# A fused gated block on one core: the feed-forward stage's operations in another order, the clip on GpSimd

## What is computed

```python
# y = layernorm(x) in bfloat16
qg, sg = dynamic_quant(y * inv_gate)      # q = clip(round(xs / scale), -127, 127), scale = max|row| / 127
qu, su = dynamic_quant(y * inv_up)
gate_out = (qg @ w_gate.T) * sg * s_wgate
up_out   = (qu @ w_up.T)   * su * s_wup
inter = clip(silu(gate_out) * up_out, -10, 10).astype(bfloat16)
qi, si = dynamic_quant(inter * inv_inter)
out = x + tanh(g_ffn) * (qi @ w_down.T) * si * s_wdown
```

## Time and profile before

| | |
|---|---|
| median of 3 executions | 1535.75 us (1533.9 to 1536.63) |
| the profiled execution | 1532.84 us, its span 1531.0 us |
| busy over the span: TensorE, VectorE, ScalarE, GpSimd | 96%, 64%, 36%, 41% |
| granted TensorE clock over the span | 0.993 of full speed |
| feed-forward stage: from the last attention output to the end | about 1380 to 1531 us |

### The profile page before, as it was taken

One profiled execution on the slowest core, in us unless ns is written; L12 is line 12 of the kernel. 1 busy time (PEld: TensorE's weight loads), 2 busy tenths in 40 slices (PEclk: granted clock), 3 DMA queues, 4 the chain that ended last, 5 costly groups with the idle time before them and its releaser, 6 DMA issues.

```text
span 1531.0 us, 19268 instructions
## 1 busy us (share of the span) xinstructions
PE 1476.8 (96%) x7475; PEld 1211.4 (79%) x7488; DVE 972.8 (64%) x1528; ACT 557.5 (36%) x862; POOL 626.8 (41%) x403
## 2 busy tenths in 40 slices
PE   7899999999999999999999999999999999997996
PEld 7878888888888888887878888888888888874553
DVE  5956565656565656666465646565656556587995
ACT  4424141314141413244451414131323232248884
POOL 3535242434343333330443433333343333225996
PEclk9999999999999999999999999999999999999999
DMA  8823131312122222218241212122112222364553
GB/s 299 239 64 92 42 92 36 97 29 82 51 77 56 77 57 61 62 51 270 90 139 29 78 41 76 44 67 51 49 48 59 57 56 64 83 220 143 187 179 138
DMA packets 193787, 142.92 MB, mean 93 GB/s; under 512 B 147744, under 2 KB 162592, under 8 KB 193312
## 3 DMA queue, kind: packets, MB, share of 16 engines
q1 hardware_dynamic: 193264, 138.54, 30.4%
q0 software_dynamic: 432, 3.15, 1.0%
HBM read 124.88 MB, written 19.92 MB: 95 GB/s over the span
## 4 chain that ended last, share of the span: by engine, by line
PE 83%; DVE 5%; ACT 4%; DMA 3%; POOL 2%; issue 2%; SPq 1%; POOLq 0%; ACTq 0%
PE psum L518 17%; PE psum L520 17%; PE psum L519 17%; PE psum L572 7%; PE psum L607 7%; PE psum L609 7%; PE psum L608 7%; PE psum L581 2%; POOL go L1220 2%; DVE sc L1507 1%; ACT xg L1008 1%; DMA wv_raw<-in_wv_t 1%; ACT xu L1009 1%; ACT xi L1013 1%; DMA wk_raw<-in_wk_t 1%
## 5 line engine op out<-in xcount | busy, mean ns | idle before, releaser
L518 PE MATMUL psum<-xt_hi,wq_hi 128*128 128x512 f32 x1024 | 405.8, 396 | 2.0 <-DVE xt_lo L1251 2.0
L520 PE MATMUL psum<-xt_hi,wq_lo 128*128 128x512 f32 x1024 | 399.7, 390 | 0.0
L519 PE MATMUL psum<-xt_lo,wq_hi 128*128 128x512 f32 x1024 | 399.5, 390 | 0.0
L1149 POOL TENSOR_TENSOR rot<-rot 128x1024 f32<-128x1024 f32 x64 | 153.8, 2403 | 429.4 <-DVE rot L1355 427.6
L1121 POOL TENSOR_TENSOR wd_lo<-wd_raw,wd_hi 128x512 fp32r<-128x512 f32 x128 | 164.4, 1290 | 252.5 <-ACT wd_hi L870 252.5
L1404 DVE TENSOR_TENSOR acc<-psum,acc 128x512 f32<-128x512 f32 x224 | 154.3, 689 | 152.8 <-PE psum L609 150.9
L906 ACT ACTIVATE vw_hi<-psum 64x512 fp32r<-64x512 f32 x256 | 151.7, 592 | 211.2 <-PE psum L520 208.0
L518 PEld LDWEIGHTS psum<-xt_hi,wq_hi 128*128 128x128 f32 x1024 | 192.9, 188 | 41.3 <-DVE xt_lo L1251 2.8
L520 PEld LDWEIGHTS psum<-xt_hi,wq_lo 128*128 128x128 f32 x1024 | 192.6, 188 | 41.2
L519 PEld LDWEIGHTS psum<-xt_lo,wq_hi 128*128 128x128 f32 x1024 | 193.1, 189 | 38.3
L1251 DVE TENSOR_TENSOR vw_lo<-psum,vw_hi 64x512 fp32r<-64x512 f32 x256 | 176.3, 689 | 72.2 <-ACT vw_hi L906 66.3
(11 more groups left out here) (135 smaller groups left out, 1986.0 us busy)
## 6 DMA issues: line engine op xcount, KB each, us to landing
wq_raw<-in_wq_t SPq DMA_DIRECT2D x128, 256.0 KB, 4.0
wd_raw<-in_wd_t SPq DMA_DIRECT2D x128, 256.0 KB, 3.1
acc<-in_x SPq DMA_DIRECT2D x16, 512.0 KB, 5.2
x_scratch<-acc SPq DMA_DIRECT2D x16, 512.0 KB, 5.0
xa<-x_scratch SPq DMA_DIRECT2D x16, 512.0 KB, 3.3
xb<-x_scratch SPq DMA_DIRECT2D x16, 512.0 KB, 4.2
out_x<-res SPq DMA_DIRECT2D x16, 512.0 KB, 2.8
xn<-in_x SPq DMA_DIRECT2D x10, 512.0 KB, 5.0
```

The source lines that it names most:

```text
L518: pe.matmul(dst, a_hi, b_hi, start=start, stop=False)
L519: pe.matmul(dst, a_hi, b_lo, start=False, stop=False)
L520: return pe.matmul(dst, a_lo, b_hi, start=False, stop=stop)
L1149: pool.tensor_tensor(rot[:, 0, :, :], rot[:, 0, :, :], rot[:, 1, :, :], ALU.add).then_inc(rope_done, 1)
```

## The change

Six things change, all in `last_outputs` of the second half and in the loops behind it:

- The clip moves from VectorE to GpSimd (`limit`), directly between the product and the multiplication by inv_inter. For the last tile VectorE does product, clip and multiplication itself (`last_inter`).
- GpSimd's `scale_up(n)` now also waits until the gate rows of the same tile are made (xg_done), and stands at the end of its step, one tile ahead: step s does gated(s-2), limit(s-2), scale_inter(s-2), add_rows(s-4), scale_up(s+1). The residual is added one step sooner than before.
- VectorE's `scale_gate` moves ahead of `gate_rows` and `up_rows`.
- TensorE turns the rows of tile 1 inside `last_outputs`, ahead of tile 0's gate and up products, each by one operation.
- VectorE does `scales(1)` ahead of the last two output additions, and ScalarE does tile 1's rounding and copying and `silu(0)` in `last_outputs`.
- `deviations`, `variances` and the second normalisation's constants are shared out over the steps in another way.

```diff
@@ -787,6 +787,11 @@
                     turn_up(0)
                 outputs(gg - 1, 14)
                 outputs(gg - 1, 15)
+                if half == 1:
+                    turn_gate(1)
+                    gate(0)
+                    turn_up(1)
+                    up(0)
 
             def keys_values(b):
 
@@ -821,7 +826,7 @@
                     slot(half, u)
                 last_outputs(half)
 
-            for s in range(1, TILES + 4):
+            for s in range(2, TILES + 4):
                 if there(s - 3):
                     down(s - 3)
                 if there(s - 1):
@@ -972,7 +977,7 @@
 
             def deviations(half, t):
                 tile = half * HTILES + t
-                act.wait_ge(mean_done, 1 if half == 0 else 2 + t // BT)
+                act.wait_ge(mean_done, 1 if half == 0 else (2, 2, 2, 2, 3, 3, 4, 4)[t])
                 if half == 0 and t == 0:
                     act.wait_ge(xt_ps, 2 * HTILES)
                 if tile:
@@ -1042,6 +1047,15 @@
                     round_rows(0)
                     deviations(1, 2)
                     deviations(1, 3)
+                    evacuate_gate(0)
+                    evacuate_up(0)
+                    round_rows(1)
+                    rows(2)
+                    deviations(1, 4)
+                    deviations(1, 5)
+                    evacuate_gate(1)
+                    silu(0)
+                    evacuate_up(1)
                 if half == 0:
                     copy_rows(1, 1)
                     normalise(3)
@@ -1094,10 +1108,10 @@
                     slot(half, u)
                 last_outputs(half)
 
-            for s in range(1, TILES + 3):
+            for s in range(2, TILES + 3):
                 if there(s - 3):
                     evacuate_inter(s - 3)
-                if there(s - 1):
+                if there(s - 1) and s > 2:
                     evacuate_gate(s - 1)
                     evacuate_up(s - 1)
                 if there(s + 1):
@@ -1108,10 +1122,9 @@
                     round_inter(s - 2)
                 if there(s - 1):
                     silu(s - 1)
-                if s < 3:
-                    deviations(1, BT + 2 * (s - 1))
-                    deviations(1, BT + 2 * (s - 1) + 1)
-                if s == 3:
+                if s < 4:
+                    deviations(1, s + 4)
+                if s == 4:
                     root(TILES + 2, slice(HTILES, TILES))
 
 
@@ -1219,6 +1232,12 @@
                 pool.wait_ge(sl_done, n + 1)
                 pool.tensor_tensor(go[:, n % 2, :], sl[:, n % 2, :], uo[:, n % 2, :], ALU.mult).then_inc(it_done, 1)
 
+            def limit(n):
+                pool.wait_ge(it_done, n + 1)
+                if there(n - 2):
+                    pool.wait_ge(xi_done, n - 1)
+                pool.tensor_scalar(ib[:, n % 2, :], go[:, n % 2, :], LIMIT, -LIMIT, ALU.min, ALU.max).then_inc(ib_done, 1)
+
             def scale_inter(n):
                 pool.wait_ge(ib_done, n + 1)
                 if there(n - 2):
@@ -1233,14 +1252,16 @@
             scale_up(0)
             scale_up(1)
             pool.wait_ge(fv_in, 32)
-            for s in range(2, TILES + 5):
-                if there(s - 5):
-                    add_rows(s - 5)
-                if there(s):
-                    scale_up(s)
-                if there(s - 2):
+            for s in range(1, TILES + 4):
+                if there(s - 2) and s - 2 < TILES - 1:
                     gated(s - 2)
+                    limit(s - 2)
                     scale_inter(s - 2)
+                if there(s - 4):
+                    add_rows(s - 4)
+                if there(s + 1):
+                    pool.wait_ge(xg_done, s + 2)
+                    scale_up(s + 1)
 
 
         @block.vector
@@ -1512,11 +1533,17 @@
                     dve.wait_ge(tg_ps, n - 1)
                 dve.tensor_tensor(xg[:, n % 2, :], yb[:, n % 2, :], v_ig[:, :], ALU.mult).then_inc(xg_done, 1)
 
-            def limit(n):
+            def last_inter(n):
+                k = n % 2
+                dve.wait_ge(sl_done, n + 1)
+                dve.wait_ge(uo_done, n + 1)
+                dve.tensor_tensor(go[:, k, :], sl[:, k, :], uo[:, k, :], ALU.mult).then_inc(it_done, 1)
                 dve.wait_ge(it_done, n + 1)
-                if there(n - 2):
-                    dve.wait_ge(xi_done, n - 1)
-                dve.tensor_scalar(ib[:, n % 2, :], go[:, n % 2, :], LIMIT, -LIMIT, ALU.min, ALU.max).then_inc(ib_done, 1)
+                dve.wait_ge(xi_done, n - 1)
+                dve.tensor_scalar(ib[:, k, :], go[:, k, :], LIMIT, -LIMIT, ALU.min, ALU.max).then_inc(ib_done, 1)
+                dve.wait_ge(ib_done, n + 1)
+                dve.wait_ge(ti_ps, n - 1)
+                dve.tensor_tensor(xi[:, k, :], ib[:, k, :], v_ii[:, :], ALU.mult).then_inc(xi_done, 1)
 
             def scales(n):
                 k = n % 2
@@ -1604,13 +1631,14 @@
                 add(gg - 1, 13)
                 if half == 1:
                     gate_greatest(1)
+                    scales(1)
+                    means(slice(HTILES + BT, HTILES + BT + 2), HALVES * GROUPS * OPG - 2)
                 add(gg - 1, 14)
                 add(gg - 1, 15)
                 if half == 0:
                     means(slice(0, HTILES), GROUPS * OPG)
                 else:
-                    means(slice(HTILES + BT, TILES), HALVES * GROUPS * OPG)
-                    scales(1)
+                    means(slice(TILES - 2, TILES), HALVES * GROUPS * OPG)
 
             def row_statistics(t):
                 dve.wait_ge(x_in[t], 16)
@@ -1665,27 +1693,29 @@
                 for u in range(UNITS):
                     slot(half, u)
                 last_outputs(half)
-            for s in range(1, TILES + 4):
+            for s in range(1, TILES + 3):
                 if there(s) and s >= 2:
-                    scale_gate(s)
                     gate_greatest(s)
-                if there(s - 2):
-                    limit(s - 2)
-                if there(s) and s >= 2:
                     scales(s)
                 if there(s - 2):
+                    if s - 2 == TILES - 1:
+                        last_inter(s - 2)
                     dve.wait_ge(xi_done, s - 1)
                     greatest(sc[:, s % 2, 6:7], xi[:, s % 2, :], imax_done)
+                    if s - 2 == TILES - 1:
+                        scale_of_inter(s - 2)
                 if there(s - 3):
                     out_rows(s - 3)
-                if there(s - 2):
+                if there(s - 2) and s - 2 < TILES - 1:
                     scale_of_inter(s - 2)
+                if there(s + 1):
+                    scale_gate(s + 1)
                 if there(s - 1):
                     gate_rows(s - 1)
                     up_rows(s - 1)
-                if s == 3:
+                if s == 4:
                     variances(slice(HTILES, TILES), TILES)
-                if s == 4:
+                if s == 5:
                     second_norm(5, 1)
 
 
```

## The result

The changed kernel takes **1539.12 us** (median of ten executions, 1538.27 to 1540.91) against 1535.22 (ten, 1533.69 to 1536.73) for the kernel before on the same chip: ratio 1.0028, 95% interval 1.0020 to 1.0035. It is slower, by 3.9 us (0.28%) where 4.3 were forecast.

The account below looks back on a forecast made before the run. VectorE was taken to bound the stage after the last attention output, 8.37 us a tile. Head +0.8, middle +4.5 and tail -1.0 sum to +4.3 us, put on the median: 1540.0 us, range 1535.5 to 1547.5.

Parts of the forecast that it names:

- VectorE would no longer be the bound: Middle tiles: VectorE loses the clip (0.34 us) and xg's collision (0.70), leaving 7.33 us of work from 8.37.
- The ring: Middle tiles: VectorE and GpSimd exclude each other and take turns, 8.25 + L, so 9.05 us a tile against 8.36.
- L: Duration of the clip on GpSimd, shown nowhere in the trace; taken as 0.80 us, with ends 0.53 and 1.27.
- the fill's end of the range: Low end for the clip's duration on GpSimd: 0.53 us, the time of the fill, which has no input.
- the case of the cheap clip: Rival: GpSimd's clip near 0.53 us, up to 0.65; total 1536.0 us, no change that can be told; chance 0.27.
- eleven rings, 99.55: Middle, between the products of tiles 0 and 14: eleven of the 14 steps at the full period, 99.55 us together.
- Head and first steps: Before and after tile 0's product: head +0.8 us; two steps without a residual or xg_done change, 7.8 and 9.0; last step 7.1.
- Tail: From tile 14's product to the end of the last residual: 20.3 us against 21.25, -1.0, with -2.3 as bound.
- the slow case: Last tile's down product at 3.22 us, granted clock 0.55, instead of 1.9; tail 20.3 us rather than 19.0.
- The residual as a term of the ring: Middle tiles: GpSimd's residual addition keeps the shared port pair 2.24 us, so gscale and xg start when it gives way.
- The rival that had the residual out of the way: Residual does not hold off xg: GpSimd 7.8 us a tile, VectorE 7.3, total 1527.5 us, faster; chance 0.06.
- The wait for xg: Middle tiles: GpSimd's up rows xu wait for VectorE's gate rows xg, counted with a hand-over of 0.08 us.

Follow-up runs that it names:

- the three accumulating kernels: Changed kernel with the residual added by an accumulating DMA, then two versions with further edits on top: 1534.46, 1533.65 and 1531.66 us.
- the transfer: Changed kernel without GpSimd's residual addition and its wait for xg; an accumulating DMA adds the down result to the output: 1534.46 us, ratio 0.9998.
- the columns: Accumulating version with VectorE's two-column scale operation done as two one-column ones and the second normalisation's constants moved between gscale and xg: 1533.65 us, ratio 0.9992.
- ScalarE's order: The accumulating version by columns, with ScalarE making yb (rows) ahead of copying out the turned gate and up rows: 1531.66 us, ratio 0.9982.

## Why the prediction was right, and where it was not

The mechanism, the sign and the size were right (1540.0 for 1539.12). That the total came so close is in part luck: one term was too large and one was missing, by about as much. Taken by its steps:

- *VectorE would no longer be the bound.* Right: 66.87 of 75.27 us, with idle time where it was named. Of the collisions it was right that xg and the product lose theirs. It did not see the new one: the operation on sc, 0.58 for 0.17, beside the clip. It is covered by the 1.06 us of idle time. With it VectorE's work a tile fell by 0.54 us (8.37 to 7.83), not by the "some 1 us" forecast.
- *The ring.* Its terms came out one by one: xi 1.12, residual and gscale 2.30 (forecast 2.30), xg with its hand-over 1.30 (1.30), xu 2.09 (2.10), product with its hand-over 1.38 (1.35). The clip done twice and the gate rows put late move the period as the sum says, by 0.68 and 1.30.
- **L was mis-sized.** "I take less, **0.80**": the clip lasts 0.61, 0.69 with its hand-over, near the fill's end of the range (0.53). Period 8.89 for 9.05. By L it was the case of the cheap clip that came true ("up to L = 0.65"), and its time, 1536.0, did not. At 15 us for each us of L the forecast's own sum gives 1537.2 for L = 0.61, 2.0 under the measured time. The clip, with one input, takes less than half of the two-input product (0.61 for 1.27) here.
- **A term was missing**, "eleven rings, 99.55": one of the eleven carries the second normalisation, 11.17 us, 2.28 over the period. The forecast took the operations on 8 columns for nothing. The other ten took 88.99 us in place of 90.5, 1.5 too much for L, and this one is 2.1 too little against 9.05. The two errors undo each other: 123.67 measured, 123.4 forecast. This is the luck in the number.
- *Head and first steps.* The first product came 0.83 us later within the stage, +0.8 forecast; then 7.70 for 7.8, 8.77 for 9.0, the last step 7.04 for 7.1.
- *Tail.* 20.55 for 20.3. The last tile's down product took 3.29 us, the slow case again, as was chosen. In four of the other kernels it took 1.90, so that this choice could have been 1.4 us off; the forecast kept that as its bound.
- *The sum against the clock.* The stage grew by 4.9 us where 4.3 were forecast, the medians of ten by 3.9. The sum was put on the median of three, 1535.75, 0.5 over that of ten.
- *The residual as a term of the ring.* Right as a number, but with less behind it than it seemed: without it the ring is 0.11 shorter. The rival that had the residual out of the way, "the ring would open", named 7.8 us a tile. The run without any residual has 8.78, so its reason was wrong, and not only its chance small: xu waits for xg, and xg for xi's greatest, with the residual or without.
- *The wait for xg* was put on the ring with the hand-over of 0.08 only. Without the wait the period is 0.22 shorter. With the clip on VectorE and the wait kept, the new order has 8.67 against 8.36 before. That is 2.5 us over the eight steps in the middle behind the normalisation, and 1.0 of it comes back in the last step (6.82 for 7.84) and 0.7 in the tail. In all the new order costs 1.3 us by the stage and 0.7 by the medians, which is within the interval. The sooner start of the second tile doesn't pay for it: alone it has the ratio 1.0001.

Of the 4.9 us by which the stage grew, the clip on GpSimd is 3.6 by the run that puts it back (3.8 without the excess of the tail): 0.22 a tile, and 1.1 in the normalisation's step (11.17 against 10.10). The Trainium skill (GPSIMD Engine Reference, "Engine selection") calls one-input work roughly line-rate, an estimate of 0.43 us here; the trace has 0.61, 40% more. By that estimate the ring's piece from the product to xi would be 1.38 + 0.51 = 1.89 us, still not under the 1.81 (1.27 + 0.54) that it has with the clip on VectorE.

What stays open: that xg wins by 0.02 us in the kernel without the wait was seen in the profiled execution alone, and whether it is so in each one is not shown. Which of its two speeds the last down product takes, and why, is open too. The intervals of the three accumulating kernels overlap from one to the next, so that the gain of the last one (3.4 us against before) is divided between the transfer, the columns and ScalarE's order by their profiles alone, one execution each. Without the excess of the tail these have stages of 171.5, 170.7 and 168.6 against 171.1 before: by them the transfer alone gains nothing, and most comes with ScalarE's order.

## What to carry to other kernels

When two engines exclude each other on a resource and also wait for each other's data, add up the ring and not the busy times: work taken off an engine on it brings only what the parallel way is shorter by (2.33 us of work gave 0.11), while a small operation put on it counts in full for each turn. Before moving an operation to relieve an engine, ask whether it stands in idle time that the rest of the change makes; here the clip was moved off VectorE at the moment at which VectorE got 1.06 us of idle time a tile. Count the small operations that occur once as well, with the collisions that they meet. And before two stages are compared by one profile each, see that their ends ran at the same clock: here that alone was 1.2 to 2.2 us, more than several of the effects looked for.

## What was unexpected of the hardware

- A tiny VectorE operation can wait for a whole GpSimd instruction: 128x2 tensor_scalar 0.17 alone, 0.58 beside the clip, 1.08 beside the residual and 1.11 beside xi; 128x8 with two SBUF inputs 0.17 alone, 0.79 beside xu. The same tensor_scalar on 128x1 took 0.14 to 0.15 in every tile, and 0.21 for two of them. The Trainium skill (SBUF — State Buffer, "Who interferes with whom") has tensor_scalar among the operations that can take the shared pair, in its two-port modes. The trace agrees for two columns, with 0.58 for 0.17; the tensor_scalar on one column was held off in no tile.
- Where two instructions ask for the pair within 0.02 us, the starts in the trace don't tell who gets it. In the kernel without the wait xg got it in all ten tiles of the middle in which it started 0.00 to 0.02 ahead of xu. In the kernel with the sooner second tile alone xg started 0.01 ahead of the product and lost, 2.37 us against 1.27.
- The last down product, with 0.69 us of idle time before it each time, took 1.90 us in four kernels (granted clock 1.00) and 3.15 to 3.60 in nine (0.50 to 0.53).
- An accumulating transfer of 512 KB holds GpSimd for 0.89 us at its issue, and lands 5.5 us after it (median of 16), against 2.33 us for the addition on the engine.
- Between GpSimd's own instructions that wait for each other lie 0.08 to 0.10 us; where they do not wait they overlap by some 0.05.
